# Routed experts beside a selective scan: the expert tiles in an even table over chunks 1 to 13, and gated rows scattered to token order instead of gathered

## The reference, cut to what matters

```python
xn = layernorm(x)                                  # x: 32 sequences x 256 tokens x 128
out = x + mamba(xn) + moe(xn)

def mamba(h):                                      # 256 inner channels, 4 heads of 64, 16 states
    x, z = split(h @ in_proj_w.T)
    x = silu(conv1d_causal(x, 4 taps) + conv_b)
    dt, B, C = split(x_proj(x))                    # by head
    delta = softplus(dt_proj(dt) + dt_proj_b)
    s[t] = s[t-1] * exp(delta[t] * A) + (delta[t] * x[t]) * B[t]     # per channel and state
    y[t] = sum_n s[t] * C[t]
    return ((y + x * Dskip) * silu(z)) @ out_proj_w.T

def moe(tokens):                                   # 8192 tokens, 8 experts, capacity 1024 each
    gates = softmax(tokens @ Wg); e = argmax(gates)
    slot = running count of the tokens of expert e; kept = slot < 1024
    row = relu(tokens @ W1[e] + b1[e]) @ W2[e] + b2[e]
    return kept * gates[e] * row
```

## Time and profile before

| what | us |
|---|---|
| median of 3 runs | 1230.49 |
| the profiled execution: time | 1231.65 |
| its span in the trace | 1229.8 |
| setup, up to the first scan | 93.6 |
| chunk 0 / chunk 1 | 91.65 / 72.38 |
| chunks 2 to 8, each | 67.8 to 69.4 |
| chunks 9 to 14, each | 68.3 to 68.8 |
| chunk 15 / after the last scan | 70.64 / 14.8 |
| busy: DVE / PE / POOL / ACT | 1065.7 / 1013.1 / 858.1 / 733.5 |

### The profile page before, as it was taken

The page is one execution under the profiler, slowest core; times in us unless marked ns, Lnnn a source line. Parts: engine busy times, 40 slices in busy tenths (PEclk is TensorE's granted clock), DMA queues, the critical chain, the costliest instruction groups (busy, mean ns, idle before and its releaser), DMA issues.

```text
span 1229.8 us, 12361 instructions
## 1 busy us (share of the span) xinstructions
PE 1013.1 (82%) x3821; PEld 476.6 (39%) x3821; DVE 1065.7 (87%) x1331; ACT 733.5 (60%) x1117; POOL 858.1 (70%) x708
## 2 busy tenths in 40 slices
PE   0755858989999899999899998798888888788775
PEld 0522314444445454444445453243343424243322
DVE  7648968889898979889898989989898989999996
ACT  2563635767585766757685866656664756556421
POOL 2335788767676867677676769687777878787755
PEclk9988878999999999999999998888898979898776
DMA  6542425243533424342534323442434342344311
GB/s 159 160 86 69 98 77 133 58 97 70 120 69 79 103 51 111 78 111 39 117 69 104 85 61 77 86 86 54 87 66 92 80 83 60 80 86 83 75 31 34
DMA packets 81089, 103.36 MB, mean 84 GB/s; under 512 B 13280, under 2 KB 51072, under 8 KB 81024
## 3 DMA queue, kind: packets, MB, share of 16 engines
q1 hardware_dynamic: 76928, 94.18, 35.4%
q0 software_dynamic: 4096, 8.40, 2.3%
HBM read 18.66 MB, written 16.78 MB: 29 GB/s over the span
## 4 chain that ended last, share of the span: by engine, by line
PE 40%; DVE 27%; issue 19%; ACT 6%; POOL 5%; DMA 1%; SPq 1%; POOLq 0%; DVEq 0%; ACTq 0%
DVE u_sb L897 11%; DVE s_sb L967 8%; PE bank L1199 5%; PE bank L1166 5%; PE bank L1184 5%; PE bank L1177 5%; PE bank L1122 3%; PE bank L1109 3%; PE bank L1130 3%; POOL s_sb L573 2%; PE bank L1142 2%; PE bank L1131 2%; PE bank L1132 2%; DVE g_sb L855 2%; DVE g_sb L859 1%
## 5 line engine op out<-in xcount | busy, mean ns | idle before, releaser
L573 POOL TENSOR_TENSOR s_sb<-s_sb,c_of 128x512 f32<-128x512 f32 x480 | 628.1, 1314 | 270.5 <-DVE s_sb L967 266.9
L967 DVE TENSOR_TENSOR_SCAN s_sb<-bank,u_sb 128x512 f32<-128x512 f32 x512 | 619.3, 1210 | 0.0
L757 ACT ACTIVATE bank<-bank,a_neg 128x510 f32<-128x510 f32 x512 | 333.6, 659 | 255.9 <-PE bank L1184 255.0
L897 DVE TENSOR_TENSOR u_sb<-bank,b_of 128x512 f32<-128x512 f32 x512 | 345.2, 674 | 100.8 <-PE bank L1177 100.8
L1177 PE MATMUL bank<-dsp,sel_d 128*128 128x512 f32 x512 | 311.1, 608 | 40.7 <-DVE u_sb L897 21.9
L1184 PE MATMUL bank<-dsp,sel_d 128*128 128x512 f32 x512 | 239.9, 469 | 82.6 <-DVE s_sb L967 77.2
L1177 PEld LDWEIGHTS bank<-dsp,sel_d 128*128 128x128 f32 x512 | 103.1, 201 | 240.4 <-DVE u_sb L897 140.2
L1184 PEld LDWEIGHTS bank<-dsp,sel_d 128*128 128x128 f32 x512 | 104.7, 205 | 196.2 <-DVE s_sb L967 168.9
L1199 PE MATMUL bank<-s_sb,con 128*32 128x512 f32 x1024 | 157.2, 690 | 12.6 <-POOL s_sb L573 8.6
L1109 PE MATMUL bank<-xnT,wx 128*128 128x512 f32 x256 | 129.0, 598 | 0.0
L580 POOL DMA_INDIRECT expert_in<-xn,put_at x64 | 65.4, 1022 | 18.0 <-issue 17.7
(11 more groups left out here) (140 smaller groups left out, 1032.1 us busy)
## 6 DMA issues: line engine op xcount, KB each, us to landing
b_of<-bc SPq DMA_DIRECT2D x64, 256.0 KB, 5.5
c_of<-bc SPq DMA_DIRECT2D x64, 256.0 KB, 5.9
dsp<-hi SPq DMA_DIRECT2D x64, 256.0 KB, 4.2
...
```

Of the source, the lines that this page charges most:

```text
L573: pool.tensor_tensor(s_now, s_now, c_of[:, hf, hh, :], ALU.mult).then_inc(S["p_ready"], 1)
L757: act.activation(d, d, ACT.Exp, scale=a_neg[:, k:k + 1]).then_inc(S["decay_ready"], 1)
L897: dve.tensor_tensor(u_sb[:, w % U_RING, :], du_ps[w % 2][:, :], b_of[:, hf, head_of(w), :], ALU.mult).then_inc(S["u_ready"], 1)
L967: dve.tensor_tensor_scan(s_sb[:, w % S_RING, :], decay_of(w)[:, :], u_sb[:, w % U_RING, :], 0.0, ALU.mult, ALU.add).then_inc(S["scan_done" ...
```

## The change

Three things change together.

1. **Rows carry gate and token.** A row of `expert_in` has 130 words: 128 of the token, its gate, and its token number. Unused slots are prefilled with token numbers in a trash area (16 fill DMAs instead of 8). Experts run in groups of 128 rows: ACT scales an output tile by the gate on its way out of PSUM, and POOL scatters it at once to a DRAM array `moe` in token order (`put_rows`). b2 comes in by a matmul with a row of ones. The gathers, DVE's bias add and DVE's gate multiply-add go away. `moe` is cleared by 8 DMAs in chunk 0, reloaded by 8 DMAs at the end of chunk 13, and added: for chunks 0 to 12 by 13 POOL adds from chunk 13 on (`add_moe`), for chunks 13 to 15 by identity matmuls in the output projection.
2. **The table of tiles.** Expert tiles (18 per expert, 144 in all) take 12 fixed places per chunk, one to a body, over chunks 1 to 13. D is spread over two bodies. Softplus steps have their own slots. Expert weights are double-buffered.
3. **Explicit banks.** Each tile names its bank; it waits for the reader of the tile before it in that bank.

```diff
-STAGE_A = {"z0": (1,), "x0": (2, 4, 5, 7), "bc0": (8,), "v0": (11,), "z1": (12,), "x1": (15, 16, 17, 17),
...
-FFN = {"xt0": (18,), "xt1": (19,), "h00": (20,), "h01": (20,), "h02": (21,), "h03": (23,),
...
-SOFTPLUS = {"act": (2, 3, 4, 5), "scale": (9,), "zero": (10,), "low": (13,), "high": (13,)}
+STAGE_A = (
+    ("x0", 1, (0, 1, 3, 4), "act", 6), ("z0", 0, (4,), "act", 5.5), ("bc0", 1, (7,), "bc", 9),
+    ("v0", 1, (9,), "act", 11), ("x1", 1, (11, 12, 13, 14), "act", 16), ("z1", 0, (13,), "act", 15.5),
+    ("D0", 0, (16, 16, 17, 17), "act", 19), ("bc1", 1, (21,), "bc", 23), ("v1", 1, (23,), "act", 25),
+    ("D1", 0, (29, 29, 31, 31), "act", 33))
+OUT_PROJ = (1, (18, 19), "dve", 20)
+FFN_AT = ((2, 0), (7, 0), (9, 0), (11, 0), (19, 0), (21, 0), (23, 0), (25, 0), (26, 1), (27, 0), (28, 1), (30, 1))
+SOFTPLUS = ({"act": (11, 12, 13, 14), "scale": (17,), "zero": (18,), "high": (22,), "low": (20,), "low_dve": (21,)},
+            {"act": (25, 26, 27, 28), "scale": (31,), "zero": (32,), "high": (36,), "low": (34,), "low_dve": (35,)})
...
+        def low_by_pool(of):
+            return of == 0 or 2 <= of <= FFN_LAST_CHUNK
...
@@ SP, setup and chunks
+            sp.wait_ge(S["fill_ready"], 1)
+            for e in range(EXP):
+                rows = ein[expert_row(e):expert_row(e + 1), :].rearrange("(p i) d -> p i d", p=P)
+                for th in range(2):
+                    sp.dma_start(rows[:, th * CT:(th + 1) * CT, :], fill_rows).then_inc(S["ein_filled"], 16)
...
             for ch in range(CHUNKS):
                 spread_bc(ch, 1)
+                if ch == 0:
+                    fill_moe()
                 stack(ch, 1)
...
+                if ch in LOAD_LATE:
+                    load_expert(LOAD_LATE[ch])
+                if ch == FFN_LAST_CHUNK:
+                    load_back()
@@ POOL
+            pool.wait_ge(S["con_loaded"], 48)
+            pool.wait_ge(S["fill_zeroed"], 1)
+            pool.tensor_copy(fill_rows[:, :, DM + 1:ROWX].bitcast(U32), trash[:, 0:CT].unsqueeze(2)).then_inc(S["fill_ready"], 1)
             for b in range(LN_BLK - 1):
...
+            def put_rows(x):
+                e, th, q = x.of, x.hf, x.k
+                pool.wait_ge(*tile_read(*x[0:4]))
+                pool.indirect_dma_start(moe[:, :],
+                                        bass.IndirectOffsetOnAxis(
+                                            ap=xe[:, e % 2, th * CT + q, DM + 1:ROWX].bitcast(U32), axis=0),
+                                        eo[:, th, q, :], None).then_inc(half_put(e, th)[0], 16)
+            def add_moe(k):
+                pool.wait_ge(*tile_read("outp", k, 0, 0))
+                pool.wait_ge(S[f"back_loaded{k * CT // GROUP}"], 16)
+                rows = acc[:, k * CT:(k + 1) * CT, :]
+                pool.tensor_tensor(rows, rows, back[:, k * CT:(k + 1) * CT, :], ALU.add).then_inc(S["moe_added"], 1)
@@ ACT
+            def expert_out(x):
+                if x.k == 0 and (x.of, x.hf) != (0, 0):
+                    act.wait_ge(*half_put(x.of - 1 + x.hf, 1 - x.hf))
+                act.wait_ge(S["misc_pe"], tile_made(*x[0:4]))
+                act.activation(eo[:, x.hf, x.k, :], misc[x.bank][:, 0:DM], ACT.Copy,
+                               scale=xe[:, x.of % 2, x.hf * CT + x.k, DM:DM + 1]).then_inc(S["misc_act"], 1)
@@ DVE
-            def expert_out(ch, th):
-                dve.tensor_tensor(eo[:, th, :, :], tile_bank(ch, f"o{th}")[:, :].rearrange("p (i d) -> p i d", d=DM),
-                                  bias.broadcast_to([P, CT, DM]), ALU.add).then_inc(S["misc_dve"], 1)
-            def combine(ch, n, extra=0):
-                return dve.scalar_tensor_tensor(rows, back[:, n, :], gate[:, bass.ds(k, 1)], rows,
-                                                ALU.mult, ALU.add)
@@ PE
+            def claim(x):
+                if x[0:4] in prior:
+                    pe.wait_ge(*tile_read(*prior[x[0:4]]))
...
+                    pe.matmul(t[:, 0:DM], one_row[0:1, :], b2_sb[0:1, b, :],
+                              start=True, stop=False)
                     for f in range(FT):
+                        mm = pe.matmul(t[:, 0:DM], hT[:, f, x.k * P:(x.k + 1) * P], w2_sb[:, b, f, :],
+                                       start=False, stop=(f == FT - 1))
```

More of the change, by code:

```diff
@@ L17 @@
 from concourse import mybir
+from collections import namedtuple
 from contextlib import ExitStack
@@ new lines, in bass_mamba_moe, with tile_bank @@
+        prior = {}
+        for b in range(2):
+            same = [x for x in plan if x.bank == b]
+            for x, y in zip(same, same[1:]):
+                assert x.slots[-1] <= y.slots[0], (x, y)
+                prior[y[0:4]] = x[0:4]
+        parts_at, reads_at = {}, {}
+        for x in plan:
+            for part, t in enumerate(x.slots):
+                parts_at.setdefault(t, []).append((x, part))
+            reads_at.setdefault(x.read, []).append(x)
+        def tile_bank(*key):
+            return misc[find[key].bank]
@@ new lines, in tile_made, with tile_read @@
+        def tile_made(*key):
+            return made[key]
+        def tile_read(*key):
+            return read[key]
+        def low_by_pool(of):
+            return of == 0 or 2 <= of <= FFN_LAST_CHUNK
+        events = {}
+        for of in range(CHUNKS):
+            for hf in range(HALVES):
+                slots = {k: tuple((of - 1) * SLOTS + w for w in v) for k, v in SOFTPLUS[hf].items()}
+                if of == 0:
+                    if hf == 0:
+                        continue
+                    slots = {k: (w,) for k, w in FIRST_SOFTPLUS.items()}
+                by_dve_ = of == 0 or not low_by_pool(of)
+                slots.pop("low" if by_dve_ else "low_dve")
+                for what, at in slots.items():
+                    for step, t in enumerate(at):
+                        events.setdefault((what, t), []).append((of, hf, step))
@@ L560, in body @@
[L560 to L562 removed]
+                    span = QUADS if ch == 0 else 1
+                    due = lambda what: [x for v in range(t - span + 1, t + 1) if w % span == span - 1
+                                        for x in softplus_now(v, what)]
                     zero_now = due("zero")
```

737 lines of the change are left out of this document (320 added, 417 removed).

## The result

The changed kernel takes **1199.1 us** (median of 4 runs, 1196.8 to 1200.3), the one before 1230.2 on the same chip: a ratio of 0.974, 95% interval 0.971 to 0.976. The direction was right, the size was not: 1134 was predicted, with 1098 to 1176 as the range. The profiled execution took 1199.06 us, with a span of 1197.3 and a mean granted clock of 0.917.

A forecast was written before the change was run, and what follows sets the result against it. PE's crowds in slots 18 to 31 were taken to bound chunks 1 to 8. From 1231.65, gains of 74.5, 10.5, 5 and 6 left 1135.6 profiled, 1134 as median; range 1098 to 1176.

The forecast's parts named there:

- DVE beside POOL: Chunks 2 to 13: each second gate operation waits half a POOL multiply, 0.65 twice, 1.3 us per chunk, between 0 and 2.5.
- An output tile at 1.1 us: PE, chunks 2 to 13: 8 records of 0.11 and a bias matmul of 0.2, about 1.1 us per output tile.
- ACT, 1.5 us per chunk: Chunks 2 to 13: silu block in body 16 makes slot 17's exponential late; cost 1.5 us, between 0 and 3.
- the running excess of the PE walk: Chunks 2 to 13: PE's body work beyond 1.71 us slots accumulates to 1.35 at most, in body 19.
- The seam, 0.9: Between chunks 2 to 13: body 30 has 2.4 us of PE work in 1.4 of room, leaving 0.9 us stall.
- POOL's pace, 0.4: Chunks 2 to 13: multiplies piling up behind `low` stall 0.4 us per chunk on average, between 0 and 5.
- the rival built on it: POOL sets the pace: scatters, `low` and waits for `high` make chunks 65.5 us, 1176 in all; chance 0.17.
- the rival on explicit banks: PE's tiles wait for their two explicit banks, expert chunks stay at 67.8 us, 1204 in all; chance 0.09.
- Setup and chunks 0 and 1, gain 10.5: Kernel start: fill copy loses 2 us, chunk 1 ends at 247 instead of 257.6; gain between 4 and 18.
- DVE then only waits for sums: Chunk 0, slot 24: DVE's 9 us stall for `low` shrinks as `zero` stands four slots earlier, leaving only sum waits.
- POOL's own walk: Chunk 1: POOL gives the products of slots 3 and 7 at about 199.8 and 206.3.
- Chunks 14 and 15: Chunks without expert tiles: chunk 14 takes 63 us, gain 5; chunk 15 takes 64.6, gain 6.

The follow-up runs named there:

- p1: Probe behind the changed kernel's last sum: one DVE operation started beside 1 to 8 back-to-back POOL multiplies; SBUF multiply 1.73 us for every n above 1.
- p2: Nineteen probes behind the changed kernel's last sum, DVE's start stepped by 0.13 us within POOL's second multiply; all 15 SBUF multiplies took 0.72 to 1.73 us.
- p3: Fifteen probes behind the changed kernel's last sum, with indirect DMAs among POOL's multiplies; DVE's SBUF multiply took 6.60 us with two DMAs ahead.
- e1: Changed kernel with the gate passed through PSUM, so no gate operation has both inputs in SBUF, second one in slot 5: 1161.0 us, 0.941 of before.
- e7: Changed kernel with only the second gate operation moved to slots 8 and 24 from 6 and 22, inputs still in SBUF: 1161.5 us.
- e8: e1 with each output tile's bias matmul given over 128 rows (zero weights but row 0) in place of one: 1146.6 us.
- e9: Changed kernel with only the bias matmul over 128 rows, DVE's long gate waits left in: 1178.7 us.
- e10: e8 with ACT reading xt and the last h one slot after their place, not two: 1134.9 us, 0.920 of before.
- e13: Changed kernel with only ACT's reads of xt and the last h one slot earlier: 1198.0 us, 0.970 of before.
- e4: e1 with POOL's 64 scatters of expert rows left out, so the experts' share is missing: 1160.0 us.
- e5: e1 with chunk 1's two `low` steps moved from DVE to POOL: 1158.8 us.
- e11: e10 with chunk 1's `low` steps moved to POOL: 1136.0 us against 1134.9.

## Why the prediction was wrong, point by point

- **"DVE beside POOL", 1.3 us per chunk, between 0 and 2.5.** This is the step that failed. It took the wait for half a POOL multiply, from one row with 1.67 us. One boundary is what a run of plain multiplies gives (p1, p2), but the change puts scatters into POOL's runs at just these slots, and a run with an indirect DMA shuts DVE out to its end (p3). Measured: 33 us in the operation itself and 38 in the kernel (e1, e7), where 15.6 were in the sum. Even the upper bound, 30 for twelve chunks, was too low: in chunks 2 to 13 the 24 operations took 49.5 us, where 15.8 would do. The remark behind it, that PSUM operands aren't held, was right in all probes. The Trainium skill's page "SBUF — State Buffer", section "Who interferes with whom", says that the loser is blocked for the whole instruction of the other engine: p1 agrees (1.73 us), in p3 it is blocked for up to five of them.
- **An output tile at 1.1 us.** The bias matmul was taken as 0.2, two records of the w2 kind. It is 0.41, and the first w2 record behind it 0.21 in place of 0.11: 1.50 in all. 0.4 times 64 is 26 us of PE over the forecast; the shape with 128 rows takes this 0.4 back (1.11) and gave 14.5 (e8) to 20.5 us (e9). A term of the sum that was mis-sized; the running excess of the PE walk, 1.35 at most, had no room for it.
- **ACT, 1.5 us per chunk.** The silu block itself was right: slots 15 and 16 take 2.4 and 2.3, together 1.3 over. But the walk put ACT's reads only before its own exponentials. That PE waits for the read of xt and of the last h, placed two slots behind while the next tile is one place behind, was no step. It costs 11.7 us once the rest is mended (e10), and between 1 and 5 beside the rest (e13).
- **The seam, 0.9:** 1.3 (slot 31 takes 2.9 to 3.0).
- **POOL's pace, 0.4, and the rival built on it:** nothing (1160.0 in e4 against 1161.0 in e1). POOL's idle time ended by scans is still 172 us. This rival gave 1176, nearer to the result than the forecast, and was yet the wrong cause: POOL's load matters by whom it locks out. The nearest number, the 1204 of the rival on explicit banks, would have been luck as well. PE does wait for ACT's reads of xt and of the last h (5.2 and 3.4 us in the whole run), but because the next matmul needs what ACT copies, not because of its bank.
- **Setup and chunks 0 and 1, gain 10.5:** 5.6 (chunk 2 starts at 252.0, before at 257.6). The fill copy held up POOL's first multiply exactly as said, answering to the earlier trace rows:
```profile
33.90 0.19 POOL L530 CAST fill<-g_sb 128x4 uint32<-128x4 f32 x1 [6.71 <-DMA g_sb<-consts]
34.04 3.60 POOL L534 TENSOR_TENSOR xn<-xn,sp_x 128x2048 f32<-128x2048 f32 x1
```
  2.0 us there, of which 1.1 reached the first scan. DVE ran free in chunk 1 from slot 4 on, but sat before `low` in slot 3, answering to the earlier trace rows:
```profile
195.56 1.23 DVE L901 TENSOR_TENSOR dd<-dd,hi 128x1024 fp32r<-128x1024 f32 x1 [8.09 <-ACT hi L738]
```
  POOL, ahead of it, and ACT:
```profile
194.34 0.10 POOL L546 MEMSET dd<- 128x2 f32 x1
194.47 1.06 ACT L738 ACTIVATE hi<-dd 128x1024 fp32r<-128x1024 f32 x1 [9.01 <-POOL dd L546]
```
  POOL's own walk was right: the product of slot 3 ended at 199.15 (199.8 forecast), that of slot 7 at 206.27 (206.3). The step that failed is "DVE then only waits for sums": `low` waits for `high`, and that for POOL's `zero` behind the scatters of chunk 0, so the scan of slot 4 came at 197.30 and the chunk ended at 252.0, not 247. Moving `low` to POOL gains nothing, since it puts 2.36 us twice onto the engine that is late (e5, e11).
- **Chunks 14 and 15, the tail, no wait on banks or on `hi`:** as predicted (chunk 15 is 1.0 shorter than said).

The miss of 65 us is closed by three mends to within 1 us: e10 takes 1134.9. That agreement is partly luck. Without any hold chunks 2 to 13 take 61.7 us each there, where my terms without the two for POOL give 60.3 (57.9 + 0.9 + 1.5). The 1.4 over is spread: slot 31 takes 2.8 to 3.3 us, slot 6 2.2 to 2.4 (DVE waits 0.4 to 0.6 us for ACT's exponential) and slot 30 up to 2.1, and the two operations of a gate take 1.39 in place of 1.27. And e10 has no hold at all, where the forecast had allowed 15.6 us for one. What stays open is why a run is let go at each boundary without an indirect DMA and not with one; the runs show the rule and not its mechanism.
